# Expert outputs scattered into token order in place of gathers in the last phase

## The chip, the cores and the metric

One core of a Trainium2 chip runs the whole program in one launch. A NeuronCore has TensorE (PE), VectorE (DVE), ScalarE (ACT), GpSimd (POOL) and SyncE (SP), each with its own stream of instructions; they meet only at semaphores. 16 DMA engines carry the transfers. The metric is the device time of the program in microseconds.

## The reference

```python
x = layernorm(x + attention(x))         # (8, 1024, 256)
x = layernorm(x + ffn(x))

def ffn(x):                             # 8 experts, 2 chosen for each token
    gates = softmax(xf @ gate_w)
    topw, topi = top_k(gates, 2);  topw = topw / sum(topw)
    h = gelu(ln(einsum('td,edh->teh', xf, w1) + b1, ln1_g, ln1_b))
    y = einsum('teh,ehd->ted', h, w2) + b2
    out = einsum('ted,te->td', y, combine)    # combine: topw at the chosen experts, 0 elsewhere
    return ln(out + xf, ln_g, ln_b)
```

There are 8192 tokens of 256 features, a hidden size of 512, and so 16384 pairs of a token and a chosen expert. The attention (16 heads, latents of 32, rotary tables, causal) is computed first and is not touched by the change, but for the routing at the end of each batch.

## The kernel before

Phases follow each other: `weight_phase` folds weights, `attention_phase` does the attention batch by batch with the routing of each batch (the order of its items is written out by hand in `PLACES`), `expert_phase` runs the experts on gathered tiles of tokens, `combine_phase` mixes the two outputs of each token and normalises. Each phase ends with a barrier of all engines.

*Routing.* For each of the 8 batches, `route_step(b, i)`, i from 0 to 21 on VectorE, finds the two experts of each token (8 tiles of 128 tokens) and the token's place in each expert's list. The place is a number of a row in the DRAM table `token_of_row` (67584 rows: 8320 for each expert, and spare ones). Step 19 stores the places in `routes["slot"]`, step 20 the token numbers in `ids`. Then 16 indirect DMAs of GpSimd (items `SCAT`, L769) write the token numbers to the table, 128 elements of 4 bytes each. The table was filled with zeros in `weight_phase`.

*Tables at the end of the routing* (L879 to L919). VectorE works out for 136 tiles of 128 rows (`MAX_TILES`: 128 full tiles and one partial one for each expert) which expert and which first row of the table each has. The experts' outputs are kept tile by tile in DRAM, `y_rows` with 136 x 128 rows, so the places in `routes["slot"]` are corrected at last to rows of `y_rows` (L902 to L912), behind a wait for all scatters. `y_rows` holds padding rows as well.

*Expert stage* (`expert_phase`). It is pipelined over the tiles k by hand, each engine with its own order. SyncE loads 128 token numbers (`tok`, L1006) up to 12 tiles ahead, GpSimd gathers the 128 rows of x1 (L984, an indirect DMA) 6 tiles ahead. TensorE transposes them (L1047), ScalarE rounds them to fp32r (`x_hi`, L1093), VectorE takes the remainder (`x_lo`, L1104), and TensorE multiplies with w1 in three products of high and low halves (L1058). VectorE adds the bias (L1113), takes statistics (L1123 to L1127), GpSimd raises the variance to the power -1/2 (L990), VectorE normalises (L1118), TensorE transposes (L1024), ScalarE applies GELU (L1076) and rounds (`g_hi`, L1080, in two halves of two column blocks). The low halves `g_lo` are the remainders: those of blocks 0 and 1 are taken by VectorE (L1130) at the end of its turn, those of blocks 2 and 3 by GpSimd (L994). TensorE multiplies with w2 (L1036), ScalarE moves the result to SBUF (`y_out`, two buffers, L1087), and SyncE stores it as a plain block of `y_rows` (L1009).

*Last phase* (`combine_phase`). It goes over 16 groups of 512 tokens (`CG` = 4 tiles), with three buffers. SyncE loads x1 (0.5 MB) and stores the output (0.5 MB) of the group three before. GpSimd gathers both outputs of each token by `routes["slot"]`, 8 indirect DMAs of 128 rows a group (L1202), a group as soon as `mixed` says that the one three before was used. TensorE sums x1 and the two outputs times their weights (L1216, L1218, `f_ps`), VectorE and ScalarE do two layer norms (L1239 to L1277, L1327), and TensorE brings in x1 and a bias (L1227, L1228).

## Time and profile before

| | us |
|---|---|
| median of 3 runs (2500.8 to 2524.76) | 2509.27 |
| the profiled execution | 2506.28 |
| its span | 2504.6 |
| TensorE, VectorE, ScalarE, GpSimd busy | 2162.4, 1672.8, 1366.1, 1373.5 |

A row of a group of instructions has its line in the kernel, engine, operation, output <- input, and count, then the busy time, the mean of one in ns, and the idle time of the engine just ahead of them with what ended it. A row of the order of time begins with the start and the duration in us. "issue" or "remote" as a cause means that the profile shows nothing that ended the wait. The expert stage lies from 1744 to 2281 us of the span, the last phase behind it.

### The profile page before, as it was taken

Reading aid. Unit: us, or ns where it says so; the run is one execution under the profiler, and the core shown is the slowest. Engines: PE = TensorE matmul, PEld = TensorE weight load, DVE = VectorE, ACT = ScalarE, POOL = GpSimd, SP = SyncE. Lnnn points to the kernel's source line nnn. Section 1 sums busy time; section 2 is a strip of 40 time slices with the busy share of each in tenths; the row PEclk is TensorE's granted clock in tenths of the full one; section 3 lists DMA queues with packets and bytes.
Section 4 is the critical chain, followed back from the end, with each engine's and each line's share of the span. In section 5 each row is a group of like instructions: output and inputs, shape, how many; then the busy total and the mean of one; then the engine's idle time right before and its main releaser. Section 6 shows DMA issues by size and latency. Waiting matters only on the chain. (4 is left out here: it accounts for less than half of the span.)

```text
span 2504.6 us, 43646 instructions
## 1 busy us (share of the span) xinstructions
PE 2162.4 (86%) x12268; PEld 1490.6 (60%) x12268; DVE 1672.8 (67%) x4866; ACT 1366.1 (55%) x3316; POOL 1373.5 (55%) x1606
## 2 busy tenths in 40 slices
PE   2698998999899999899899899940999999996876
PEld 2454655555555555556556566430888888885665
DVE  2476687686577687677677678434777777773676
ACT  0155655555545565564564566621677777773333
POOL 1455465664654754763674675415566666665562
PEclk7799999998898898998998999865999999998898
DMA  3556556556545555564565565250222222223563
GB/s 116 129 123 146 120 119 155 113 120 142 124 100 133 118 130 136 120 136 120 125 131 128 119 128 129 49 199 7 65 71 71 71 71 70 70 71 105 158 185 114
DMA packets 192967, 284.06 MB, mean 113 GB/s; under 512 B 55752, under 2 KB 113760, under 8 KB 192608
## 3 DMA queue, kind: packets, MB, share of 16 engines
q1 hardware_dynamic: 173664, 238.18, 40.0%
q0 software_dynamic: 16768, 34.69, 4.8%
q10 hardware_dynamic: 2304, 8.39, 0.9%
q8 instruction: 110, 1.80, 0.3%
q14 instruction: 121, 0.99, 0.2%
HBM read 99.41 MB, written 37.56 MB: 55 GB/s over the span
## 5 line engine op out<-in xcount | busy, mean ns | idle before, releaser
L515 ACT ACTIVATE probs<-scores_T 128x512 f32<-128x512 f32 (+3 forms) x1536 | 654.5, 492 | 258.5 <-PE scores_T L405 245.9
L748 POOL TENSOR_SCALAR_AFFINE_SELECT probs<-probs 128x256 f32<-128x256 f32 x512 | 205.6, 410 | 544.4 <-ACT probs L515 541.7
L463 PE MATMUL ring<-k_stack,q_stack_b 96*128 96x512 f32 (+3 forms) x1024 | 403.5, 437 | 19.4 <-DVE neg_part L660 9.1
L660 DVE TENSOR_REDUCE neg_part<-ring 128x1 f32<-128x512 f32 x512 | 333.2, 683 | 96.5 <-PE ring L463 93.5
L405 PE MATMUL scores_T<-q_stack_b,k_stack 98*128 98x512 f32 (+3 forms) x1024 | 328.3, 398 | 46.5 <-ACT probs L515 45.8
L422 PE MATMUL o_ps<-probs,v_ones 128*17 128x512 f32 (+3 forms) x3072 | 350.7, 530 | 1.9 <-POOL probs L748 1.7
L463 PEld LDWEIGHTS ring<-k_stack,q_stack_b 96*128 96x128 f32 x1024 | 196.7, 201 | 228.9 <-issue 84.8
L665 DVE CUSTOM_DVE_ANT_0 ring<-ring,mask 128x384 f32<-128x384 f32 (+3 forms) x512 | 243.3, 507 | 116.7 <-PE ring L463 114.5
L665 DVE CUSTOM_DVE_ANT_0 ring<-ring,mask,neg_part 128x384 f32<-128x384 f32 (+3 forms) x512 | 260.7, 554 | 83.6 <-PE ring L463 83.3
L1076 ACT ACTIVATE o_sb<-ht_ps,ln_b,ln_g 128x128 f32<-128x128 f32 x544 | 217.1, 449 | 114.7 <-PE ht_ps L1024 76.4
L405 PEld LDWEIGHTS scores_T<-q_stack_b,k_stack 98*128 98x128 f32 x1024 | 193.3, 206 | 104.0 <-ACT probs L515 79.5
L445 PE MATMUL ring<-x_hi,lat_w 128*128 128x512 f32 x512 | 189.1, 412 | 29.4 <-DVE x_lo L637 29.4
L523 ACT ACTIVATE u<-ring,lat_bias 128x512 f32<-128x512 f32 x128 | 87.8, 688 | 205.3 <-PE ring L445 190.0
L463 PE MATMUL ring<-k_stack,q_stack_a 96*128 96x384 f32 (+3 forms) x512 | 172.3, 371 | 24.5 <-DMA k_stack<-u_rot 20.4
L732 POOL TENSOR_TENSOR u<-u,cos 128x512 f32<-128x512 f32 x128 | 164.6, 1286 | 40.4 <-DMA u_rot<-u 40.1
L990 POOL TENSOR_TENSOR h_rstd<-h_ve,minus_half 128x1 f32<-128x1 f32 x136 | 91.4, 672 | 173.1 <-DVE h_ve L1127 173.1
L740 POOL TENSOR_TENSOR u<-u,u_rot 128x512 f32<-128x512 f32 x128 | 164.6, 1286 | 9.7 <-POOL u_rot L735 0.4
L1036 PE MATMUL y_ps<-w_hi,g_hi 128*128 x544 | 165.6, 304 | 3.0 <-DVE g_lo L1130 1.5
L769 POOL DMA_INDIRECT token_of_row<-ids,slot x128 | 140.9, 1101 | 48.9 <-DVE ids_f L621 25.7
L735 POOL TENSOR_TENSOR u_rot<-u_rot,sin 128x512 f32<-128x512 f32 x128 | 166.2, 1298 | 0.1
L984 POOL DMA_INDIRECT z<-x,tok x136 | 137.4, 1010 | 41.4 <-issue 25.6
L1202 POOL DMA_INDIRECT y<-y_rows,slot x128 | 121.0, 946 | 67.1 <-issue 35.3
(192 smaller groups left out, 4682.2 us busy)
## 6 DMA issues: line engine op xcount, KB each, us to landing
u_rot<-u SPq DMA_DIRECT2D x128, 256.0 KB, 3.7
k_stack<-u_rot SPq DMA_DIRECT2D x128, 256.0 KB
y_rows<-z SPq DMA_DIRECT2D x136, 128.0 KB
lat_w<-lat_split SPq DMA_DIRECT2D x32, 512.0 KB
q_stack_a<-u_rot SPq DMA_DIRECT2D x64, 256.0 KB
q_stack_b<-u_rot SPq DMA_DIRECT2D x64, 256.0 KB
k_stack<-u SPq DMA_DIRECT2D x64, 256.0 KB
x_raw<-in_xT SPq DMA_DIRECT2D x16, 512.0 KB, 4.9
```

Of the source, the lines that this page charges most:

```text
L405: nc.tensor.matmul(sc[(t + j) % 3][:, HALF - w:HALF], k_stack[:, n % 2, h, P * kb:P * kb + P], q_stack[c][:, row_buf(n, c), h, q0 - HALF * ...
L422: last = nc.tensor.matmul(o_ps[32 * h:32 * h + VW, q0 - HALF * c:HALF], v_ones[:, b % 2, kb, HG * g + h, :], probs[:, s % 2, h, cols], sta ...
L445: last = nc.tensor.matmul(out[:], lat_w[:, kc, side, w_, :], a[:, kc, cols], start=i == 0, stop=i == 5)
L463: nc.tensor.matmul(out[:, 0:k1 - k0], q_stack[qb // 4][0:3 * L, row_buf(n, qb // 4), h, P * (qb % 4):P * (qb % 4) + P], k_stack[0:3 * L, n ...
L515: nc.scalar.activation(probs[:, s % 2, h, cols], sc[(t + j) % 3][:, HALF - w:HALF], ACT.Exp).then_inc(exp_done, 1)
L660: nc.vector.tensor_reduce(neg_part[:, n % 2, part_col], src[:], AX_X, ALU.max, negate=True).then_inc(max_taken, 1)
L665: nc.vector.tensor_tensor_reduce(out=src[:, 0:w], in0=src[:, 0:w], in1=consts["mask"][:, HALF - w:HALF], scale=-1.0, scalar=neg_part[:, n ...
L732: nc.gpsimd.tensor_tensor(u[s][:, cols], u[s][:, cols], consts["cos"][:, cols], ALU.mult).then_inc(cos_done[s], 1)
L735: nc.gpsimd.tensor_tensor(u_rot[s][:, cols], u_rot[s][:, cols], consts["sin"][:, cols], ALU.mult).then_inc(sin_done[s], 1)
L748: nc.gpsimd.affine_select(both, both, [[0, 2], [1, P]], ALU.is_ge, zero, base=0, channel_multiplier=-1).then_inc(kept, 1)
L1036: nc.tensor.matmul(y_ps[j % 2][:, 0:C], a[j % 2][:, f, :], experts[w][:, bass.ds(e, 1), C * f:C * f + C], start=f == 0 and a is g_hi and w ...
L1076: nc.scalar.activation(g[k % 2][:, f, :], ht_ps[k % 2][:, P * f:P * f + P], ACT.Gelu, bias=experts["ln1_b"][:, f, bass.ds(e, 1)], scale=ex ...
```

## The change

The row table has two numbers for each row: the token, and the row of the output table `y_rows`, which is now in token order: row t for the first choice of token t, 8192 + t for the second, and one more row, 16384, for all padding. The routing scatters both numbers. In the expert stage GpSimd scatters each tile's 128 result rows to these rows (two tiles later in its order, four buffers), and each scatter waits until the one before it has landed. SyncE no longer stores results there and only loads row numbers, up to 16 tiles ahead. VectorE takes both low halves: the first ahead of the statistics, the second behind them. The last phase loads y as plain blocks on SyncE, and GpSimd does nothing in it. The correction of the places goes, as do `routes["slot"]` and the tables it used.

```diff
-            nc.vector.memset(zero_ids[:], 0).then_inc(zero_set, 1)
+            nc.vector.memset(no_token[:, :, 0], 0).then_inc(zero_set, 1)
+            nc.vector.memset(no_token[:, :, 1], 2 * B * T).then_inc(zero_set, 1)
...
-                return nc.vector.tensor_copy(routes["slot"][:, :, TB * b:TB * b + TB], slot_f[:])
+                return nc.vector.tensor_copy(slot[:], slot_f[:])
...
-                    if i == 20 and n:
+                    if i == 19 and n:
                         dve.wait_ge(scattered, 16 * 2 * TB * n)
...
-                    j = TB * n + tb
                     nc.gpsimd.indirect_dma_start(
-                        token_of_row, bass.IndirectOffsetOnAxis(routes["slot"][:, k, j:j + 1], 0),
-                        ids[:, tb:tb + 1], None).then_inc(scattered, 16)
+                        token_of_row, bass.IndirectOffsetOnAxis(slot[:, k, tb:tb + 1], 0),
+                        ids[:, k, tb, :], None).then_inc(scattered, 16)
...
-                slots_by_expert = [P, 2 * TILES, E]
-                slots = routes["slot"][:].rearrange("p k t -> p (k t)")
-                then(nc.vector.tensor_copy(all_f[:], slots))
-                then(nc.vector.tensor_tensor(beyond, all_f[:].unsqueeze(2).to_broadcast(slots_by_expert),
-                                             next_base[:].unsqueeze(1).to_broadcast(slots_by_expert), ALU.is_ge))
-                then(nc.vector.tensor_tensor(beyond, beyond, delta[:].unsqueeze(1).to_broadcast(slots_by_expert),
-                                             ALU.mult))
-                then(nc.vector.tensor_reduce(skip[:], beyond, AX_X, ALU.add))
-                then(nc.vector.tensor_tensor(skip[:], all_f[:], skip[:], ALU.subtract))
-                dve.wait_ge(scattered, 16 * 2 * TILES)
-                nc.vector.tensor_copy(slots, skip[:])
...
-            for k in range(-6, MAX_TILES):
+            for k in range(-6, MAX_TILES + 2):
                 if tile(k + 6):
                     j = k + 6
-                    pool.wait_ge(tok_loaded[j % 8], 16 * (j // 8 + 1))
+                    pool.wait_ge(tok_loaded[j % 4], 16 * (j // 4 + 1))
                     if j >= 4:
                         pool.wait_ge(xt_full, j - 3)
                     nc.gpsimd.indirect_dma_start(x_in[j % 4], None, x1_rows,
-                                                 bass.IndirectOffsetOnAxis(tok[:, j % 8:j % 8 + 1], 0)
+                                                 bass.IndirectOffsetOnAxis(tok[:, j % 16, 0:1], 0)
                                                  ).then_inc(x_in_loaded[j % 4], 16)
                 if tile(k + 2):
                     j = k + 2
                     pool.wait_ge(ve_done, j + 1)
                     nc.gpsimd.tensor_tensor(h_rstd[j % 2][:], h_ve[j % 2][:], routes["minus_half"][:],
                                             ALU.pow).then_inc(rstd_done, 1)
-                if tile(k):
-                    pool.wait_ge(g_hi_ready, 2 * k + 2)
-                    nc.gpsimd.tensor_tensor(g_lo[k % 2][:, pairs[1], :], g[k % 2][:, pairs[1], :],
-                                            g_hi[k % 2][:, pairs[1], :].bitcast(F32),
-                                            ALU.subtract).then_inc(g_lo2_ready, 1)
+                if tile(k - 2):
+                    j = k - 2
+                    pool.wait_ge(y_ready, j + 1)
+                    if j:
+                        pool.wait_ge(y_stored[(j - 1) % 4], 16 * ((j - 1) // 4 + 1))
+                    nc.gpsimd.indirect_dma_start(y_rows, bass.IndirectOffsetOnAxis(tok[:, j % 16, 1:2], 0),
+                                                 y_out[j % 4], None).then_inc(y_stored[j % 4], 16)
+            for a in range(4):
+                pool.wait_ge(y_stored[a], 16 * (MAX_TILES // 4))
 
         @block.sync
         def _(sp):
-            for k in range(-12, MAX_TILES):
-                if tile(k + 12):
-                    j = k + 12
-                    row = sp.value_load(routes["row"][0:1, j:j + 1], min_val=0, max_val=ROWS - P)
-                    if j >= 8:
-                        sp.wait_ge(x_in_loaded[j % 4], 16 * (j // 4 - 1))
-                    sp.dma_start(tok[:, j % 8:j % 8 + 1], token_of_row[bass.ds(row, P), :]).then_inc(tok_loaded[j % 8], 16)
-                if tile(k):
-                    sp.wait_ge(y_ready, k + 1)
-                    sp.dma_start(y_rows[P * k:P * k + P, :], y_out[k % 2]).then_inc(y_stored[k % 2], 16)
-            for a in range(2):
-                sp.wait_ge(y_stored[a], 16 * HALF_TILES)
+            for j in range(MAX_TILES):
+                row = sp.value_load(routes["row"][0:1, j:j + 1], min_val=0, max_val=ROWS - P)
+                if j >= 4:
+                    sp.wait_ge(tok_loaded[j % 4], 16 * (j // 4))
+                if j >= 16:
+                    sp.wait_ge(y_stored[j % 4], 16 * (j // 4 - 3))
+                sp.dma_start(tok[:, j % 16, :], token_of_row[bass.ds(row, P), :]).then_inc(tok_loaded[j % 4], 16)
+            for a in range(4):
+                sp.wait_ge(tok_loaded[a], 16 * (MAX_TILES // 4))
...
-                        pe.wait_ge((g_lo_ready, g_lo2_ready)[i], j + 1)
+                        pe.wait_ge(g_lo_ready, 2 * j + i + 1)
...
-                    if j >= 2:
-                        act.wait_ge(y_stored[j % 2], 16 * (j // 2))
-                    nc.scalar.activation(y_out[j % 2], y_ps[j % 2][:, 0:C], ACT.Identity).then_inc(y_ready, 1)
+                    if j >= 4:
+                        act.wait_ge(y_stored[j % 4], 16 * (j // 4))
+                    nc.scalar.activation(y_out[j % 4], y_ps[j % 2][:, 0:C], ACT.Identity).then_inc(y_ready, 1)
...
+            def split_g(k, i):
+                part = pairs[i]
+                dve.wait_ge(g_hi_ready, 2 * k + i + 1)
+                nc.vector.tensor_tensor(g_lo[k % 2][:, part, :], g[k % 2][:, part, :],
+                                        g_hi[k % 2][:, part, :].bitcast(F32), ALU.subtract).then_inc(g_lo_ready, 1)
...
                                             h_rstd[j % 2][:, 0:1], ALU.subtract, ALU.mult).then_inc(h_norm_ready, 1)
+                if tile(k):
+                    split_g(k, 0)
...
                     nc.vector.tensor_scalar(h_ve[j % 2][:], h_mv[j % 2][:, 1:2], EPS, None, ALU.add).then_inc(ve_done, 1)
                 if tile(k):
-                    dve.wait_ge(g_hi_ready, 2 * k + 1)
-                    nc.vector.tensor_tensor(g_lo[k % 2][:, pairs[0], :], g[k % 2][:, pairs[0], :],
-                                            g_hi[k % 2][:, pairs[0], :].bitcast(F32),
-                                            ALU.subtract).then_inc(g_lo_ready, 1)
+                    split_g(k, 1)
...
                     sp.dma_start(x1[n % 3][:], tiles_of(x1_dram)[n]).then_inc(x1_loaded[n % 3], 16)
+                    for k in range(2):
+                        src = tiles_of(y_rows[B * T * k:B * T * (k + 1), :])[n]
+                        sp.dma_start(y[k][n % 3][:], src).then_inc(y_loaded[n % 3], 16)
...
-        @block.gpsimd
-        def _(pool):
-            for n in range(n_groups):
-                if n >= 3:
-                    pool.wait_ge(mixed, CG * (n - 2))
-                for t in range(CG):
-                    for k in range(2):
-                        nc.gpsimd.indirect_dma_start(
-                            y[k][n % 3][:, t, :], None, y_rows,
-                            bass.IndirectOffsetOnAxis(routes["slot"][:, k, CG * n + t:CG * n + t + 1], 0)
-                        ).then_inc(y_loaded[n % 3], 16)
...
-                pe.wait_ge(y_loaded[n % 3], 16 * 2 * CG * (n // 3 + 1))
+                pe.wait_ge(y_loaded[n % 3], 16 * 2 * (n // 3 + 1))
...
-    token_of_row = nc.dram_tensor("token_of_row", (ROWS, 1), I32).ap()
-    y_rows = nc.dram_tensor("y_rows", (MAX_TILES * P, C), F32).ap()
+    token_of_row = nc.dram_tensor("token_of_row", (ROWS, 2), I32).ap()
+    y_rows = nc.dram_tensor("y_rows", (2 * B * T + 1, C), F32).ap()
```

## Rows read from the trace of the kernel before

**Rows 1.** Busy time of each engine by stretch: expert stage, last phase.

```profile
core 0: us, PE busy (x) PEld busy (x) DVE busy (x) ACT busy (x) POOL busy (x), PEclk, DMA share, GB/s
1900.00:2250.00 350.00, 344.89 (x2297) 304.14 (x2296) 262.40 (x644) 264.77 (x736) 220.16 (x276) 1.00 0.25 71
...
2340.00:2400.00 60.00, 50.43 (x225) 41.78 (x224) 42.62 (x187) 25.47 (x75) 38.83 (x42) 1.00 0.59 178
```

**Rows 2.** Groups of instructions of the expert stage; first GpSimd's low half alone.

```profile
L994 POOL TENSOR_TENSOR g_lo<-o_sb,g_hi x136: 714/729/743, 1764.8 to 2276.4; 128x256 fp32r<-128x256 f32 x136
...
L984 POOL DMA_INDIRECT z<-x,tok x79 | 80.0, 1012 | 15.7 <-issue 15.7
...
L1130 DVE TENSOR_TENSOR g_lo<-o_sb,g_hi 128x256 fp32r<-128x256 f32 x79 | 32.9, 416 | 0.0
```

**Rows 3.** Order of time, one tile of the expert stage.

```profile
2031.40 0.60 PE L1024 MATMUL ht_ps<-ident,h_norm 128*128 128x128 f32 x4
...
2032.92 0.68 DVE L1123 BATCH_NORM_STATS2 h_stats<-h_norm 128x6 f32<-128x512 f32 x1
...
2032.99 0.42 ACT L1080 ACTIVATE g_hi<-o_sb 128x256 fp32r<-128x256 f32 x1
...
2034.99 0.60 PE L1024 MATMUL ht_ps<-ident,h_norm 128*128 128x128 f32 x4
```

**Rows 4.** Order of time, start of the last phase.

```profile
2290.55 0.95 POOL L1202 DMA_INDIRECT y<-y_rows,slot  x1 [0.30 <-issue]
...
2293.45 1.19 PE L1216 MATMUL f_ps<-x,ident 128*128 128x256 f32 x2 [14.97 <-DMA y<-y_rows,slot]
```

**Rows 5.** SyncE: last stores of the expert stage; its waits (total, times, longest).

```profile
2276.59 2.65 SPq L1009 DMA_DIRECT2D y_rows<-z  x2
...
SPq L375 <- DMA inv_sums<-inv: 106.5, 27, 7.5
...
SPq L1011 <- DMA y_rows<-z: 1.4, 1, 1.4
```

**Rows 6.** Order of time, end of the routing.

```profile
1708.82 11.42 DVE L720 TENSOR_TENSOR w_lo<-w_lo,w_hi 128x1024 fp32r<-128x1024 f32 x10
1708.84 12.38 POOL L769 DMA_INDIRECT token_of_row<-ids,slot  x1 [0.30 <-issue]
...
1731.61 0.96 POOL L769 DMA_INDIRECT token_of_row<-ids,slot  x1 [0.31 <-issue]
1742.50 0.23 DVE L912 CAST slot<-skip 128x128 int32<-128x128 f32 x1 [18.02 <-DMA token_of_row<-ids,slot]
...
1743.45 0.22 DVE L916 TENSOR_TENSOR weight<-weight,w_tmp 128x64 f32<-128x64 f32 x1
```

**Rows 7.** The last phase: a wait in total, the gathers' line, order of time.

```profile
DVE c_stats L1239 <- remote: 41.3, 10, 12.6
...
L1202 POOL DMA_INDIRECT y<-y_rows,slot x128: 940/946/1000, 2281.7 to 2464.3; - x128
...
2298.53 0.76 DVE L1239 BATCH_NORM_STATS2 c_stats<-f_ps 128x6 f32<-128x256 f32 x2 [16.93 <-issue]
...
2326.73 1.65 DVE L1268 SCALAR_TENSOR_TENSOR v<-v,c_rstd,xb_ps 128x256 f32<-128x256 f32 x4 [11.04 <-issue]
...
2363.65 0.94 POOL L1202 DMA_INDIRECT y<-y_rows,slot  x1 [1.99 <-remote]
...
2375.33 0.94 POOL L1202 DMA_INDIRECT y<-y_rows,slot  x1 [1.99 <-remote]
...
2468.15 1.66 DVE L1268 SCALAR_TENSOR_TENSOR v<-v,c_rstd,xb_ps 128x256 f32<-128x256 f32 x4 [9.44 <-issue]
...
2484.16 1.65 DVE L1262 SCALAR_TENSOR_TENSOR v<-f_ps,c_mv,ln_g_rep 128x256 f32<-128x256 f32 x4
...
2489.12 0.76 DVE L1239 BATCH_NORM_STATS2 c_stats<-f_ps 128x6 f32<-128x256 f32 x2
...
2492.80 1.65 DVE L1262 SCALAR_TENSOR_TENSOR v<-f_ps,c_mv,ln_g_rep 128x256 f32<-128x256 f32 x4
```

More of the change, by code:

```diff
@@ L79, in _ @@
                 sp.dma_start(dst[:], dram[name]).then_inc(loaded, 16)
-            sp.wait_ge(zero_set, 1)
-            sp.dma_start(token_of_row.rearrange("(p s) o -> p (s o)", p=P), zero_ids[:]).then_inc(zeroed, 16)
+            sp.wait_ge(zero_set, 2)
+            sp.dma_start(token_of_row.rearrange("(p s) o -> p s o", p=P), no_token[:]).then_inc(zeroed, 16)
             sp.wait_ge(split, 1)
@@ L194, in attention_phase @@
         before, ones, chosen, first, second = (tail[k] for k in ("before", "ones", "chosen", "first", "second"))
-        top, best, slot_f, ids_f, ids = (tail[k] for k in ("top", "best", "slot_f", "ids_f", "ids"))
+        top, best, slot_f, slot, ids_f, ids = (tail[k] for k in ("top", "best", "slot_f", "slot", "ids_f", "ids"))
         flat = lambda m: m.rearrange("p t e -> p (t e)")
@@ L956, in expert_phase @@
         g_lo = [sb(f"g_lo{a}", [P, FC, P], F32R) for a in range(2)]
-        y_out = [tail["z"][:, 4 + a, :] for a in range(2)]
+        y_out = [tail["z"][:, 4 + a, :] for a in range(4)]
         ps = lambda name: [ctx.enter_context(nc.psum_tensor(f"{name}{a}", [P, HALF], F32)) for a in range(2)]
         xt_ps, h_ps, ht_ps, y_ps = ps("xt_ps"), ps("h_ps"), ps("ht_ps"), ps("y_ps")
-        tok = sb("tok", [P, 8], I32)
-        tok_loaded = [sem(f"tok_loaded{a}") for a in range(8)]
+        tok = sb("tok", [P, 16, 2], I32)
+        tok_loaded = [sem(f"tok_loaded{a}") for a in range(4)]
         x_in_loaded = [sem(f"x_in_loaded{a}") for a in range(4)]
-        y_stored = [sem("y_stored0"), sem("y_stored1")]
+        y_stored = [sem(f"y_stored{a}") for a in range(4)]
         xt_full, xe_hi_ready, xe_lo_ready, h_full = sem("xt_full"), sem("xe_hi_ready"), sem("xe_lo_ready"), sem("h_full")
@@ L1070, in _ @@
                     if k >= 2:
-                        act.wait_ge(g_lo_ready, k - 1)
-                        act.wait_ge(g_lo2_ready, k - 1)
+                        act.wait_ge(g_lo_ready, 2 * (k - 1))
                         act.wait_ge(y_full, k - 1)
@@ L1367, in build @@
         sb = lambda name, shape, dt=F32: ctx.enter_context(nc.sbuf_tensor(name, shape, dt))
-        routes = {"ident": sb("ident", [P, P]), "weight": sb("weight", [P, 2, TILES]),
-                  "slot": sb("slot", [P, 2, TILES], I32)}
+        routes = {"ident": sb("ident", [P, P]), "weight": sb("weight", [P, 2, TILES])}
         tail = tail_buffers(ctx, nc)
```

17 lines of the change are left out of this document (8 added, 9 removed).

## The prediction

> **What bounds the kernel now.** I read the busy time by stage first [rows 1]. In the expert stage TensorE is busy 344.9 of 350 us and its clock is granted at 1.00 (2.4 GHz), while VectorE, ScalarE and GpSimd are at 63 to 76%. In the last phase no engine passes 85% (TensorE 50.4 of 60 us) and the DMA engines stand at 0.59. So the expert stage is bound by TensorE's stream and the last phase by something else.
>
> The groups of instructions of the expert stage [rows 2] give its beat: GpSimd's low half starts 136 times between 1764.8 and 2276.4, so a tile takes 511.6 / 135 = 3.79 us. The order of time inside one tile [rows 3] shows TensorE going from one set of transposes (2031.40) to the next (2034.99) in 3.59 us with no idle time, beside ScalarE and VectorE, which wait for it.
>
> The last phase is read from three places. In its middle GpSimd starts a batch of 8 gathers at 2363.65 and the next at 2375.33, a group every 11.68 us, and waits 1.99 us between batches [rows 7]. VectorE waits 41.3 us in all, in 10 waits, for something that the profile can't name, and twice more stands still, 11.04 and 9.44 us, just before 2326.73 and 2468.15 [rows 7]. Once the gathers are over (the last starts at 2464.3), the same code does a group in 2492.80 - 2484.16 = 8.64 us [rows 7]. The chain of waits, followed back, lies almost wholly in this phase.
>
> **The change, part by part.**
>
> *The last phase loses its 128 gathers.* From the first statistics of group 0 (2298.53) to those of group 15 (2489.12) it takes 190.6 us [rows 7]. Without gathers every group should go as the last ones do: 15 x 8.64 = 129.6 us, so **-61.0 us**. The bounds: at best this (the order of TensorE's and VectorE's instructions doesn't change), at worst the named waits stay and nothing is gained. I take the full sum because the unnamed waits and the two standstills all lie beside gathers and none lies behind the last one. Cover: the loads. A group moves x1, two y blocks and its output, 4 x 0.52 = 2.1 MB. At 178 GB/s the DMA engines are busy 0.59 [rows 1], which makes 302 GB/s at full share, so 6.9 us for a group, under 8.64. If that cover failed, a group would be bound by the transfers; at twice the cost per byte, 13.9 us, the phase would lose 32 us on before instead of winning.
>
> *Its start.* Now TensorE begins at 2293.45, 2.9 us behind the start of the eighth gather at 2290.55 [rows 4]. After, SyncE issues two 0.13 MB and three 0.52 MB loads, at about the time of the first gather, 2281.7 [rows 7]: 1.8 MB at 302 GB/s are 6.0 us, and about 2 us from issue to the last landing (the plain store takes 1.7 [rows 5]), so 2290: **-3.5 us** (bounds -6 and 0). SyncE then issues four DMAs a group in place of two; it waits for output n-3 before it loads n+1, which leaves two groups, 17 us, for a load.
>
> *Expert stage, the scatter.* SyncE's store of a tile goes, and GpSimd gets an indirect DMA; nothing of before writes 1 KB rows this way. For the issue I take a gather's 1.0 us [rows 2]. GpSimd is busy 220.2 of 350 us [rows 1], 2.38 us a tile; less the low half's 0.73 plus 1.0 that is 2.65, and with some 0.3 us ahead of each indirect DMA about 3.2 of 3.79. It fits. But a scatter isn't issued before the one ahead of it has landed, so the landing time L, from its start, sets a floor under the beat. Behind that wait stand the next tile's gather and the power that VectorE's normalisation waits for. The gather, on the same queue and with the same rows and bytes, lands in 2.9 us [rows 4]. The lower bound is the plain store, 0.3 + 1.4 = 1.7 us [rows 5]; the upper one the token scatter of 4-byte elements, whose last started at 1731.61 and freed VectorE at 1742.50, 10.9 us [rows 6]. I take 2.9, the row nearest in queue, row size and bytes: under 3.79, so **0** in the steady beat. With the upper end it would be 136 x 7.1 = +967 us.
>
> The Trainium skill, "DMA: Bandwidth & Descriptors", section "Anatomy of one DMA — SWDGE (gpsimd) path", gives about 2.0 us plus bytes / 436e3 for such a DMA; by an estimate from that page L would be 2.3 us and the term 0 as well, but its section puts most of the 2 us on the receipt of the target memory and calls HBM the heaviest, which speaks for more in this direction.
>
> *Expert stage, the low half.* GpSimd's 0.73 us becomes a second 0.42 us on VectorE [rows 2]. VectorE goes from 262.4 / 350 x 3.79 = 2.84 to 3.26 us a tile, 86%. The first one now stands ahead of the statistics: it must wait for ScalarE's rounding, which ends at 2032.99 + 0.42 = 2033.41, where the statistics started at 2032.92 [rows 3]. So statistics and everything behind them, the variance that GpSimd waits for included, come 0.5 + 0.4 = 0.9 us later. The normalisation, whose end the statistics followed at 2032.92, is over 2.0 us before the transposes that read it start at 2034.99 [rows 3], so these are not late: **0** (below: a gain of 0.05 us a tile at most, for TensorE has no more idle time [rows 1]; above: the second rival).
>
> *End of the expert stage.* The last two stores start at 2276.59 and about 2278.9, and the last is in 1.4 us behind 2279.24, at 2280.6 [rows 5]. Now the last scatter waits for the one before it: that can start at 2276.6, lands at 2279.5, and the last lands at 2282.4: **+2 us** (bounds 0 and, by the landing rival, 7). SyncE's token loads run up to 16 tiles ahead and stay hidden.
>
> *Routing.* After the last token scatter VectorE did a cast and three more steps, 1742.50 to 1743.67 [rows 6]; these run earlier now: **-1.2 us**. Five table steps on VectorE lay under the scatters: 0. The token scatter carries 8 bytes instead of 4, 128 descriptors either way: 0 taken, bounds -1 and +2. The wait that moves one step ahead is for scatters of the batch before, long over: 0. The zero table of twice the size lies beside the weight loads: 0.
>
> **The sum**: -61.0 - 3.5 + 2 - 1.2 = -63.7 us on the profiled execution's 2506.28 (span 2504.6 and 1.7 around it) gives 2442.6. The median of the runs is 3.0 above that execution, so 2446.
>
> **Rivals.**
>
> *Landing bound (slower).* The place is GpSimd's wait ahead of each scatter. For: stores to HBM of short rows in the attention stage let SyncE wait 106.5 us in 27 waits, 3.9 us each and up to 7.5, behind the issue [rows 5], and the token scatter took 10.9. With 0.95 of issue L is 4.9 us, the beat too, and the stage grows by 136 x 1.1 = 151 us: 2597. It decides from L = 3.79 + 63.7 / 136 = 4.26 us on. Against: those rows are 4 and 128 bytes, these 1 KB.
>
> *GpSimd and VectorE in each other's way (gain shrinks).* VectorE ran ten subtractions with both inputs in SBUF, 11.42 us from 1708.82; GpSimd's indirect DMA of 1708.84 took 12.38 us instead of 0.96 [rows 6]. The change puts two such subtractions a tile beside two indirect DMAs. If each blocks GpSimd for its 0.42 us, GpSimd needs 3.2 + 0.84 = 4.04 us, 0.25 over the beat: +34 us, 2480. Against: GpSimd idles before the power, so that blocks mostly eat idle time. The Trainium skill, "SBUF — State Buffer", section "Who interferes with whom", states that a VectorE instruction with two SBUF inputs and a GpSimd one that reads SBUF exclude each other. The trace agrees with it.
>
> *The last phase's waits stay.* The 1.99 us and the unnamed waits might come from the plain loads, which also end with the gathers. Then a group keeps some 3 us of waits: 15 x 3 = 45 us less gain, 2491. Against: GpSimd, which touches none of these loads, waits in the same places.
>
> **Numbers.** The forecast 0.62, its own range 2434 to 2462; landing bound 0.14; GpSimd against VectorE 0.14; waits stay 0.10. A 1% change is 25 us, about what a measurement tells from none. Faster by over 1% is the forecast, two thirds of the second rival and a third of the third: 0.62 + 0.09 + 0.03 = 0.74. Slower is the landing rival, 0.14. Within 1% is the rest, 0.12. The range reaches from 2434 (start and end of the phases at their good ends, a few us less in the last phase) to 2491, and leaves out the landing rival and part of the third, 0.19.
>
> **What would show it.** In the changed profile: the last phase at 8.6 us a group and without unnamed waits; the expert stage at 3.79 us a tile with GpSimd waiting little for its own scatters; statistics on VectorE starting right behind the first low half. A beat near the scatter's landing time, with GpSimd waiting for a DMA ahead of each scatter, would prove me wrong, as would a last phase with a busy share of the DMA engines near 1.

## The result and the profile after

The changed kernel takes **2413.88 us** in the median (2398.45 to 2421.28, 4 runs) beside 2509.91 for the kernel before (2500.8 to 2524.76, 4 runs) on the same chip: a ratio of 0.963 with the 95% interval 0.957 to 0.969. It is faster by 3.7%, and by 32 us more than I had forecast (2446). The time lies under my range, which began at 2434. The profiled execution took 2408.44 us, with a span of 2406.7. (Of the 11 runs of the kernel before beside experiments 5, 6 and 10, one ran at a granted clock of 0.80 in place of 0.91 to 0.93 and is left out of their range.)

These are the busy times by stage of the changed kernel, in the columns of [rows 1]:

```profile
1850.00:2200.00 350.00, 348.37 (x2383) 314.91 (x2382) 303.08 (x763) 276.00 (x765) 261.23 (x286) 1.00 0.25 74
2260.00:2320.00 60.00, 60.00 (x280) 52.82 (x279) 53.94 (x231) 28.57 (x85) 0.00 (x0) 1.00 0.69 218
```

In these 60 us of the last phase TensorE is now busy all of the time, on 280 products where there were 225, and GpSimd does nothing. In the expert stage TensorE's busy time rises by 3.5 us only, but the **number** of its instructions in 350 us rises from 2297 to 2383, by 3.7%. That is what I had not expected.

The next rows (line, engine, operation, tiles, count, shortest, median and longest in ns, first and last start) give the beat of the expert stage, the scatter and the statistics of the last phase:

```profile
L1118 DVE BATCH_NORM_STATS2 h_stats<-h_norm x136: 679/686/695, 1727.7 to 2220.4; 128x6 f32<-128x512 f32 x136
...
L984 POOL DMA_INDIRECT y_rows<-z,tok x136: 959/1057/1321, 1743.4 to 2237.9; - x136
...
L1222 DVE BATCH_NORM_STATS2 c_stats<-f_ps x64: 412/420/433, 2260.2 to 2392.6; 128x6 f32<-128x256 f32 x64
```

(2220.4 - 1727.7) / 135 = 3.65 us a tile, where the kernel before took 3.79 by [rows 2]. The end of the expert stage, in order of time, shows GpSimd's last scatters, ScalarE's last y_out and SyncE's first load of the last phase:

```profile
2228.50 0.38 ACT L1074 ACTIVATE z<-y_ps 128x256 f32<-128x256 f32 x1 [1.45 <-PE y_ps L1027]
...
2230.32 0.96 POOL L984 DMA_INDIRECT y_rows<-z,tok  x1 [2.98 <-DMA y_rows<-z,tok]
2234.02 0.96 POOL L984 DMA_INDIRECT y_rows<-z,tok  x1 [2.75 <-DMA y_rows<-z,tok]
2237.88 0.96 POOL L984 DMA_INDIRECT y_rows<-z,tok  x1 [2.90 <-DMA y_rows<-z,tok]
...
2246.44 0.35 SPq L1172 DMA_DIRECT2D ln_g_rep<-in_ln_g  x1
...
2254.92 1.19 PE L1199 MATMUL f_ps<-x,ident 128*128 128x256 f32 x2 [26.46 <-DMA y<-y_rows]
```

From the end of the last y_out, 2228.88, to the next phase it takes 17.6 us; in the kernel before it was 2.2 (2278.89 to 2281.10).

Where the 97.9 us between the two spans lie, by the same marks in both traces:

| stretch | before | after | difference | forecast |
|---|---|---|---|---|
| start to the first token scatter of the last batch | 1699.4 | 1678.5 | -21.0 | 0 |
| from there to the first x gather (routing) | 48.65 | 40.33 | -8.3 | -1.2 |
| to the last tile's h_norm transposes | 524.4 | 504.1 | -20.3 | 0 |
| to the end of the last y_out | 6.5 | 6.0 | -0.4 | 0 |
| to SyncE's first load of the last phase | 2.2 | 17.6 | +15.4 | +2 |
| to the first statistics | 17.4 | 13.8 | -3.7 | -3.5 |
| to the end | 206.1 | 146.5 | -59.6 | -61.0 |

All but the first row together, called "the rest" below, went from 805.2 to 728.2 us: -77.0, where I forecast -63.7.

### The profile page after: what moved, and what is told of

It reads as the page before. It is cut to its first block and busy times, and to the rows that moved or that the text cites. A ratio compares the mean times of both kernels' runs of the same rounds, so it can differ in the third digit from the quotient of the medians.

```text
span 2406.7 us, 43666 instructions
## 1 busy us (share of the span) xinstructions
PE 2111.4 (88%) x12268; PEld 1473.2 (61%) x12268; DVE 1718.2 (71%) x4997; ACT 1365.9 (57%) x3316; POOL 1302.6 (54%) x1478
## 5 line engine op out<-in xcount | busy, mean ns | idle before, releaser
L749 POOL TENSOR_SCALAR_AFFINE_SELECT probs<-probs 128x256 f32<-128x256 f32 x512 | 206.1, 411 | 529.1 <-ACT probs L516 526.1
L661 DVE TENSOR_REDUCE neg_part<-ring 128x1 f32<-128x512 f32 x512 | 333.5, 684 | 97.9 <-PE ring L464 94.8
L406 PE MATMUL scores_T<-q_stack_b,k_stack 98*128 98x512 f32 (+3 forms) x1024 | 321.0, 389 | 46.0 <-ACT probs L516 44.5
L423 PE MATMUL o_ps<-probs,v_ones 128*17 128x512 f32 (+3 forms) x3072 | 344.3, 522 | 1.8 <-POOL probs L749 1.6
L984 POOL DMA_INDIRECT y_rows<-z,tok x136 | 146.9, 1080 | 71.8 <-issue 28.2
L1024 PE MATMUL y_ps<-w_hi,g_lo 128*128 x544 | 154.0, 283 | 0.0
```

What stands on the lines that cost most here:

```text
L406: nc.tensor.matmul(sc[(t + j) % 3][:, HALF - w:HALF], k_stack[:, n % 2, h, P * kb:P * kb + P], q_stack[c][:, row_buf(n, c), h, q0 - HALF * ...
L423: last = nc.tensor.matmul(o_ps[32 * h:32 * h + VW, q0 - HALF * c:HALF], v_ones[:, b % 2, kb, HG * g + h, :], probs[:, s % 2, h, cols], sta ...
L661: nc.vector.tensor_reduce(neg_part[:, n % 2, part_col], src[:], AX_X, ALU.max, negate=True).then_inc(max_taken, 1)
L749: nc.gpsimd.affine_select(both, both, [[0, 2], [1, P]], ALU.is_ge, zero, base=0, channel_multiplier=-1).then_inc(kept, 1)
L1024: nc.tensor.matmul(y_ps[j % 2][:, 0:C], a[j % 2][:, f, :], experts[w][:, bass.ds(e, 1), C * f:C * f + C], start=f == 0 and a is g_hi and w ...
```

## The experiments

Medians on one chip are told beside the time of the kernel before on that chip. Since the attention phase ahead of it varies by tens of us from run to run, the rest of the profiled execution is the sharper number.

**1. Both low halves on VectorE, alone (e1).** What gave the faster beat? Where TensorE loses time in the kernel before is seen by its own starts, here in one tile, with GpSimd's work beside it:

```profile
2038.19 0.68 POOL L990 TENSOR_TENSOR h_rstd<-h_ve,minus_half 128x1 f32<-128x1 f32 x1 [1.56 <-DVE h_ve L1127]
2038.85 0.73 POOL L994 TENSOR_TENSOR g_lo<-o_sb,g_hi 128x256 fp32r<-128x256 f32 x1
...
2040.65 0.38 PE L1047 MATMUL xt_ps<-ident,z 128*128 128x128 f32 x2
2041.25 0.49 PE L1058 MATMUL h_ps<-w_hi,xe_hi 128*128 x1 [0.21 <-issue]
```

From the x transposes to the first W1 product it takes 0.60 us here and 0.17 in the tile before it (2036.98 to 2037.15). Only 0.21 us of it counts as idle, because the ends of products are modelled. The product's start lies 1.67 us behind the end of the low half, 2039.58. Of the 126 tiles between 1780 and 2260 us, 79 have such a gap of over 0.22 us (the others stand at 0.14 in the median), and in these 79 the product comes 1.66 us behind GpSimd's low half in the median. Together they lose 21 us. The edit on the kernel before:

```
-                if tile(k):                                # GpSimd
-                    pool.wait_ge(g_hi_ready, 2 * k + 2)
-                    nc.gpsimd.tensor_tensor(g_lo[k % 2][:, pairs[1], :], ...)
...
+                if tile(k):                                # VectorE, ahead of the statistics
+                    split_g(k, 0)
...
+                    split_g(k, 1)                          # behind them
```

> The kernel before with both low halves on VectorE and nothing else of the change. Theory A, late release: in the kernel before, 72 of 117 steady tiles let TensorE stand between its x transposes and the first W1 product (0.32 us there on average against a floor of 0.14), and that product comes 1.66 us behind the end of GpSimd's low half, so the low half, queued on GpSimd behind the power, is what TensorE's queue waits for. On VectorE it comes earlier: the beat falls from 3.79 to 3.60 to 3.66 us, the expert stage by 18 to 26 us, its end and the last phase stay as before, the time is 2484 to 2492. Theory B: the faster beat of the changed kernel comes from SyncE's order or from fewer stores; then the beat stays at 3.79 and the time at about 2510. Theory C, VectorE is late (86% busy): beat above 3.85, time above 2520.

2482.37 us beside 2509.02, ratio 0.989 (0.984 to 0.993); the rest is 777.2 us, -28.0. The beat, by the statistics' first and last start, is (2260.8 - 1774.7) / 135 = 3.60:

```profile
L1125 DVE BATCH_NORM_STATS2 h_stats<-h_norm x136: 680/686/696, 1774.7 to 2260.8; 128x6 f32<-128x512 f32 x136
```

Busy times in its expert stage, in the columns of [rows 1]:

```profile
1850.00:2200.00 350.00, 350.00 (x2427) 319.83 (x2426) 304.51 (x777) 280.14 (x778) 160.80 (x194) 1.00 0.26 75
```

2427 instructions in 350 us against 2297: TensorE now goes at the pace of the shortest tile of before, 3.59 us [rows 3], and 5 gaps are left, which lose 0.9 us in all. Theory A holds, with a little more gain than it named, and B and C fall: VectorE is at 87%, and the beat hasn't grown.

**2. The changed kernel with the low half back on GpSimd (e2).**

```
                 if tile(k + 2): ... power ...
+                if tile(k):
+                    pool.wait_ge(g_hi_ready, 2 * k + 2)
+                    nc.gpsimd.tensor_tensor(g_lo[k % 2][:, pairs[1], :], ...).then_inc(g_lo2_ready, 1)
                 if tile(k - 2): ... scatter ...
```

> The changed kernel with the second low half of each tile on GpSimd again, between the power and the scatter. Theory A: the beat goes from 3.65 back to 3.79 or more; GpSimd would have 0.96 + 0.68 + 0.73 + 1.06 us of work and about 0.2 ahead of each DMA, 3.9 us a tile, so 3.9 to 4.2, and the time rises by 35 to 75 us to 2450 to 2490. Theory B (the low half is not what made the beat faster): 3.60 to 3.66 and 2414.

2465.16 us (ratio 0.982, 0.980 to 0.985), the rest 765.5, +37.3 on the changed kernel. GpSimd, in order of time:

```profile
1951.32 1.06 POOL L989 DMA_INDIRECT y_rows<-z,tok  x1 [0.18 <-issue]
1952.68 0.97 POOL L971 DMA_INDIRECT z<-x,tok  x1 [0.30 <-issue]
1953.69 0.68 POOL L977 TENSOR_TENSOR h_rstd<-h_ve,minus_half 128x1 f32<-128x1 f32 x1
1954.35 0.72 POOL L981 TENSOR_TENSOR g_lo<-o_sb,g_hi 128x256 fp32r<-128x256 f32 x1
1955.24 1.06 POOL L989 DMA_INDIRECT y_rows<-z,tok  x1 [0.18 <-issue]
```

It waits for nobody and goes round in 1955.24 - 1951.32 = 3.92 us; the mean beat is 3.93. So with the scatter alone GpSimd would have been the bound, and the two edits belong together.

**3. The low half ahead of the power, still on GpSimd (e6).** The kernel before with these two exchanged:

```
+                if tile(k): ... low half ...
                 if tile(k + 2): ... power ...
-                if tile(k): ... low half ...
```

> The kernel before with two instructions of GpSimd exchanged: the second low half of tile k comes ahead of the power of tile k+2, and stays on GpSimd. Theory A (it is the time at which the low half ends, 1.66 us ahead of the first W1 product, that holds TensorE): ScalarE's rounding ends at about the same time as the variance, so the low half ends 0.65 us earlier; the largest stall is 0.46 us, so nearly all of them go: a beat of 3.60 to 3.65, the time 2482 to 2492. The power comes 0.7 us later, which VectorE's normalisation stands. Theory E (it is the engine: GpSimd's subtraction slows VectorE or the gather): the beat stays at 3.79, 2509.

2484.22 us beside 2506.74 (ratio 0.993, 0.988 to 0.998), the rest 787.5, -17.7. The beat is (2251.2 - 1753.6) / 135 = 3.69, half of the way and short of theory A's 3.60 to 3.65; TensorE's gaps fall from 21 us to 8. So an earlier end of the low half gives this half of the gain with the engine unchanged, and theory E, by which the beat stays, falls. What is left shows where the two engines start at once; first all 136 halves (shortest, median, longest in ns), then one tile in order of time:

```profile
L989 POOL TENSOR_TENSOR g_lo<-o_sb,g_hi x136: 731/803/1016, 1761.6 to 2258.5; 128x256 fp32r<-128x256 f32 x136
```

```profile
1949.43 0.41 DVE L1130 TENSOR_TENSOR g_lo<-o_sb,g_hi 128x256 fp32r<-128x256 f32 x1
...
1949.43 1.01 POOL L989 TENSOR_TENSOR g_lo<-o_sb,g_hi 128x256 fp32r<-128x256 f32 x1 [1.15 <-ACT g_hi L1080]
```

Beside VectorE's half GpSimd's takes up to 1.02 us in place of 0.73. All 38 halves of over 0.85 us overlap one of VectorE's, and 33 of the 44 tiles (of 126, counted as above) that still let TensorE stand come behind such a long half. That looks like the exclusion of my second rival, here between two subtractions; that it makes all of the stalls left is not shown. The Trainium skill, "SBUF — State Buffer", section "Who interferes with whom", says that a VectorE instruction with two SBUF inputs excludes a GpSimd one that reads SBUF; this trace agrees.

**4. The last phase without gathers, alone (e3).** The kernel before with two plain loads a group:

```
+                    for k in range(2):
+                        src = tiles_of(y_rows[B * T * k:B * T * (k + 1), :])[n]
+                        sp.dma_start(y[k][n % 3][:], src).then_inc(y_loaded[n % 3], 16)
...
-        @block.gpsimd
-        ...
```

> The kernel before, whose last phase loads two plain blocks of the expert results a group in place of 8 gathers (the rows are then in the wrong order, so its output is not the reference's); the expert stage is untouched. Theory A, the gathers made the waits: 8.6 to 8.8 us a group, the first to the last group's statistics in about 131 us in place of 190.6, the start 4 us earlier, together -63 us: 2444 to 2450. Theory B, the waits come from the plain loads or stores: 11 us a group or more, 2480 to 2510.

2438.86 us, ratio 0.974 (0.969 to 0.979); the rest 739.9, -65.3. From the first statistics to the end it takes 146.5 us as in the changed kernel, and the beat of the expert stage stays at 3.80. So without the gathers the last phase is that of the changed kernel: theory A. (About 2 us of the 65.3 are the routing's, 46.5 us here and 48.65 in the kernel before.)

**5. Half of the gathers (e9).** The first expert's rows gathered, the second's loaded:

```
+                    sp.dma_start(y[1][n % 3][:], tiles_of(y_rows[0:B * T, :])[n]).then_inc(x1_loaded[n % 3], 16)
...
-                    for k in range(2):
+                    for k in range(1):
                         nc.gpsimd.indirect_dma_start(y[k][n % 3][:, t, :], ...)
```

> The kernel before, whose last phase gathers only the first expert's rows (4 gathers a group) and loads the second's as one plain block a group (so rows in the wrong order, and its output is not the reference's). Theory A, GpSimd's queue is the last phase's bound: 8 x 1.25 = 10 us of issue and 1.7 of waiting make 11.68; with 4 gathers it is 5 and 1.7, 6.7, under TensorE's 8.64, and a group takes 8.6 to 8.9. Theory F, each gather holds the others up: half of the excess stays, 10.2 us a group.

2430.26 us in one run. GpSimd starts a group of four at 2336.59, 2345.23 and 2353.86: 8.64 us, TensorE's own pace, and the rest is 741.9. Theory A. This chip, however, was another than those before, and of a different kind, as the next runs show.

**6. The changed kernel again (e10), and the kernel before again (e12, e13).**

> The changed kernel once more, unaltered. Theory N, the attention phase's 21 us are chance: none of its instructions before the last batch's token scatter differ in a way that matters; in the traces of five kernels with the old routing code that scatter began between 1677.3 and 1719.5 us, in those of five with the new one between 1674.2 and 1706.6. What is left is 77 us behind that point, so the ratio is about 0.969 and the time 2425 to 2435 beside 2505 to 2510. Theory S, the attention phase gains too: the ratio is 0.963 or less.

2411.88 us (6 runs), but the kernel before took only 2460.79 in the median on this chip (2436.76 to 2469.52): a ratio of 0.980 (0.975 to 0.985). Neither theory had that. The rest of the changed kernel, 725.7 us, is as it was. Its attention phase ended at 1691.5, 13 us later than in the first trace of the same code.

> The kernel before, unaltered, for its trace. On one chip all its times were 2437 to 2470 us, on three others 2487 to 2525, while the changed kernel took 2394 to 2427 on that chip and 2398 to 2421 on the first. Something in the kernel before depends on the chip and has gone with the change. Theory L, it is the last phase with its 8 gathers a group (standstills of 9 to 11 us and waits that the profile can't name): on a chip where the time is under 2475, the phase from its first statistics on takes 165 to 185 us, on one where it is over 2485 it takes 200 to 206; the expert stage has a beat of 3.79 and the routing 46.3 to 48.7 us on either. Theory M, it is the attention phase: the last batch's token scatter begins before 1665 on a fast chip, and the last phase takes 205 us on all.

> The kernel before once more, unaltered, in the hope of the chip on which it took 2437 to 2470 us. Theory L: under 2475 us the last phase takes 165 to 185 us from its first statistics on, over 2485 us 200 to 206 us, beat and routing as ever. Theory M: the attention phase ends before 1665 on a fast chip and the last phase takes 205 us on all.

The first of the two fell on a slow chip (2504.14 us), the second on a fast one (2463.94). First and last gather and statistics on the fast one, then GpSimd in order of time there, then on the slow one:

```profile
L1202 POOL DMA_INDIRECT y<-y_rows,slot x128: 942/946/999, 2280.5 to 2439.3; - x128
L1239 DVE BATCH_NORM_STATS2 c_stats<-f_ps x64: 411/420/433, 2296.6 to 2448.1; 128x6 f32<-128x256 f32 x64
```

```profile
2329.29 0.94 POOL L1202 DMA_INDIRECT y<-y_rows,slot  x1 [0.30 <-issue]
2330.54 0.95 POOL L1202 DMA_INDIRECT y<-y_rows,slot  x1 [0.30 <-issue]
```

```profile
2345.74 0.95 POOL L1202 DMA_INDIRECT y<-y_rows,slot  x1 [0.30 <-issue]
2348.85 0.95 POOL L1202 DMA_INDIRECT y<-y_rows,slot  x1 [2.16 <-remote]
...
2357.62 0.95 POOL L1202 DMA_INDIRECT y<-y_rows,slot  x1 [0.30 <-issue]
2360.62 0.95 POOL L1202 DMA_INDIRECT y<-y_rows,slot  x1 [2.05 <-remote]
```

On the fast chip gather follows gather every 1.25 us without a break: 8 x 1.25 = 10.0 us a group, and 165.6 us from the first statistics to the end. On the slow one it is 11.77 (2348.85 to 2360.62), and 206.4. Beat (3.79 on both), routing (46.3 and 45.8) and attention (1700.7 and 1699.5) don't differ: theory L. So some 20 of the 40 us between the two are the waits of 2 us a group, and the rest two standstills of VectorE, 9.0 and 8.8 us, which the fast chip's trace hasn't. One slow chip was met twice, and stayed of its kind (2509.02 us, later 2521.48); what makes a chip of the one kind or the other is open.

> The kernel of the half gathers again (first expert's rows gathered, the second's loaded as plain blocks in the wrong order), for a chip on which the kernel before takes over 2485 us. On such chips its last phase shows 11.68 us a group and standstills, on the faster kind 10.0 us, GpSimd's 8 x 1.25. Theory A: with 4 gathers a group the queue of gathers has slack, late notices are covered, and a group takes 8.6 to 8.9 us on this kind of chip too. Theory R: the late notices go with every gather and hold up each group by 1 to 2 us whatever the queue: 9.6 to 10.7 us.

That was a fast chip once more (2439.96 us beside 2461.28). The same kernel again:

> The same kernel of the half gathers, still for a chip of the slower kind. Theory A: 8.6 to 8.9 us a group there too. Theory R: 9.6 to 10.7 us.

Now the kernel before took 2521.48 on the same chip, and the half gathers 2431.07. A group takes 8.63 us (2346.06 to 2354.69 to 2363.32), without one unnamed wait. What stands between the groups is 3.94 us in which GpSimd waits for TensorE. So the waits cost nothing once the queue of gathers has such a pause: theory A. Whether they are gone then or only covered by it is not shown.

**7. The width of the token rows (e5).** The kernel before with a two-column table:

```
-    token_of_row = nc.dram_tensor("token_of_row", (ROWS, 1), I32).ap()
+    token_of_row = nc.dram_tensor("token_of_row", (ROWS, 2), I32).ap()
...
-                        ids[:, tb:tb + 1], None).then_inc(scattered, 16)
+                        ids[:, tb, :], None).then_inc(scattered, 16)
```

> The kernel before with a row table of two columns (both hold the token), so that each token scatter writes 8 bytes a row in place of 4 and each token load reads 8; the gathers of the last phase and everything else stay. From the last token scatter to the first x gather it took 16.5, 14.1 and 14.3 us in the three kernels with 4-byte rows so far, and 8.0 to 8.2 in the three with 8-byte rows. Theory W, the width of the row: 4-byte rows land slowly; then about 10 us here (1.2 us of VectorE's last steps still lie in it). Theory O, the order: VectorE's wait with its steps behind it makes the difference; then 14 to 16 us as before. The expert stage keeps its beat of 3.79 in both.

2472.72 us in one run. From the last token scatter to the first x gather 7.9 us, theory W, and the routing 40.15 us in all:

```profile
1709.50 0.96 POOL L769 DMA_INDIRECT token_of_row<-ids,slot  x1 [0.30 <-issue]
...
1712.15 0.23 DVE L912 CAST slot<-skip 128x128 int32<-128x128 f32 x1 [9.79 <-DMA token_of_row<-ids,slot]
```

With 8 bytes a row the last scatter is in after 2.65 us, with 4 after 10.9 [rows 6].

**8. A scratch row for each row without a token (e4).** The edit on the changed kernel:

```
-            nc.vector.memset(no_token[:, :, 1], 2 * B * T).then_inc(zero_set, 1)
+            nc.gpsimd.iota(no_token[:, :, 1], pattern=[[1, ROWS // P]], base=2 * B * T,
+                           channel_multiplier=ROWS // P).then_inc(zero_set, 1)
...
-    y_rows = nc.dram_tensor("y_rows", (2 * B * T + 1, C), F32).ap()
+    y_rows = nc.dram_tensor("y_rows", (2 * B * T + ROWS, C), F32).ap()
```

> The changed kernel in which each row of the table that has no token names a scratch row of its own, in place of one row for all. Theory P, rows of padding that all write to one row land slowly: the last scatters land in 3.2 us each in place of 3.7 to 3.9 and the last one well under the 8.5 us that passed from its start to the next phase; the stretch from the last y_out on ScalarE to the next phase's first load falls from 17.5 us to 12 or less, and the time by 4 to 7 us. Theory Q, the tail is the two tiles by which the scatter lags and the chain of landings: 17 us stay, time 2412 to 2416.

2424.15 us, ratio 0.966 (0.963 to 0.969). The tail, from the end of the last y_out to the next phase, is 16.1 us; in the changed kernel it was 17.6 in the first trace and 16.2 in the second. GpSimd's last three scatters:

```profile
2252.90 0.96 POOL L988 DMA_INDIRECT y_rows<-z,tok  x1 [3.51 <-DMA y_rows<-z,tok]
2256.05 0.96 POOL L988 DMA_INDIRECT y_rows<-z,tok  x1 [2.18 <-DMA y_rows<-z,tok]
2259.21 0.96 POOL L988 DMA_INDIRECT y_rows<-z,tok  x1 [2.20 <-DMA y_rows<-z,tok]
```

They follow each other after 3.15 and 3.16 us. With one row for all padding the last two landings took 3.70 and 3.86 us in both traces of the changed kernel and 3.72 and 3.86 in experiment 2, and from the last start to the next phase it is 7.9 us here and 8.6 in those three. So the landing part of theory P holds, 0.5 to 0.7 us for each of these scatters. Its size doesn't: another landing took 4.47 us (2248.43 to 2252.90), and the tail is no shorter than in the second trace. For the time Q stands, though it came out 8 us over Q's numbers: the attention phase ended at 1701.1, and the rest, 726.0, is that of the changed kernel.

**9. No wait for the scatter before (e7), and SyncE waiting for the last (e8).** On top of experiment 8:

```
-                    if j:
-                        pool.wait_ge(y_stored[(j - 1) % 4], 16 * ((j - 1) // 4 + 1))
```

and for e8 on top of that:

```
-            for a in range(4):
-                pool.wait_ge(y_stored[a], 16 * (MAX_TILES // 4))
...
+            for a in range(4):
+                sp.wait_ge(y_stored[a], 16 * (MAX_TILES // 4))
```

> The changed kernel with a scratch row of its own for each row of the table without a token (so no two rows of any scatter coincide), and without GpSimd's wait for the scatter before: a scatter is issued as soon as its tile is ready. Theory T, the chain of landings makes part of the tail: the last scatter then starts at about the end of the last y_out, in place of 8 to 9 us later, and the tail falls from 17.6 or 16.1 to 8 to 10 us; the beat from 3.65 to 3.60 to 3.63. Together 8 to 13 us under e4: 2411 to 2416. Theory U, landings pile up: the scatters then land later each and the tail stays over 14 us.

> As e7, but the wait for the last scatters is SyncE's, and GpSimd ends its part of the phase behind the last issue. After the changed kernel's last scatter the DMA engines are idle from 2240.0 us on, and the next phase begins only at 2246.4. Theory G, GpSimd's own end of the phase takes some 5 us once its last wait is over: here it runs beside the landing and the tail falls by 2 to 4 us more than in e7. Theory H, the landing is told late: the same as e7 within 1 us.

Without the chain 2409.5 us (ratio 0.962, 0.956 to 0.968), with SyncE's wait 2399.96 (0.959, 0.954 to 0.964), beside 2506.74. The beat is 3.61 in both, the tail 8.1 and 6.4 us, the rest 712.6 and 711.0. In the trace of e7 the last scatter starts 0.3 us behind the end of the last y_out (2218.77), and the next phase 7.8 us later:

```profile
2219.05 0.96 POOL L986 DMA_INDIRECT y_rows<-z,tok  x1 [0.88 <-ACT z L1076]
...
2226.89 0.35 SPq L1174 DMA_DIRECT2D ln_g_rep<-in_ln_g  x1
```

So the chain of landings cost 8.7 us at the end (2237.88 against 2228.88 + 0.3) and 0.04 us a tile before it: theory T. Another 0.7 us of the tail is the last landing, on rows of its own (experiment 8). GpSimd's own end of the phase costs 1.7 us, under the 2 to 4 of theory G and over the 1 of theory H.

**10. The best version (e11).** On top of that, SyncE's loads of group 0 go ahead of the two norm vectors:

```
-            sp.dma_start(g_rep[:], dram["ln_g"]).then_inc(gb_loaded, 16)
-            sp.dma_start(b_rep[:], dram["ln_b"]).then_inc(gb_loaded, 16)
...
+                    if n == 0:
+                        sp.dma_start(g_rep[:], dram["ln_g"]).then_inc(gb_loaded, 16)
+                        sp.dma_start(b_rep[:], dram["ln_b"]).then_inc(gb_loaded, 16)
```

> As e8 (scratch rows for padding, no wait for the scatter before, SyncE waits for the last scatters), and in the last phase SyncE loads x1 and the two y blocks of group 0 ahead of the two vectors of the norm. In the changed kernel the y block is issued 1.3 us after SyncE's first load and lands 6.5 us later, and TensorE starts on it. Theory A, the landing follows the issue: TensorE starts 0.8 to 0.9 us earlier in the phase, and the time is 17 to 20 us under the changed kernel's: 2405 to 2415. Theory D, the DMA engines are full with the five loads: no gain at the start.

2398.42 us (6 runs) beside 2411.88 for the changed kernel on the same chip; against the kernel before 0.977 (0.973 to 0.982) and 0.980 (0.975 to 0.985). These intervals overlap; the rest, 709.9 against 725.7, shows 15.8 us, nearly all of it experiment 9's (711.0). TensorE starts 7.5 us behind SyncE's first load, 8.35 in e8 and 8.5 in the first trace of the changed kernel: theory A, though the gap of the medians, 13.5 us, is under its 17 to 20.

## Why the prediction was wrong

The miss by the two profiled executions is 97.9 - 63.7 = 34.2 us: 21.0 from the attention phase, 20.3 from the expert stage's beat and 7.1 from the routing on the one side, 13.4 from the stage's end on the other; the other rows give back 0.8.

**The last phase (-61.0) and its start (-3.5)** were right in mechanism and size: -59.6 and -3.7, and a group at 2391.26 - 2382.63 = 8.63 us. What I could not see in one trace is that 40 of these 60 us belong to a kind of chip: on the other kind the gathers cost only their queue, 10.0 us a group, and the last phase would have won 165.6 - 146.5 = 19 us. That the forecast came out here is so in part luck: it was compared on a chip of the kind that its trace came from. I had taken the unnamed waits into the sum because none lay behind the last gather. That reading held, also on the slow kind with half of the gathers. One bound was miscounted: at 13.9 us a group 15 groups would have lost 15 x 13.9 - 190.6 = 18 us, not 32.

**The low half, "0 (below: a gain of 0.05 us a tile at most, for TensorE has no more idle time)"**, is the step that failed. The term is mis-sized: alone it gains 0.19 us a tile, 27.0 us from the first x gather to the last transposes (experiment 1), and 20.3 in the changed kernel, where the scatters take some back. I bounded it by TensorE's idle time, 350 - 344.9 us [rows 1]. But the ends of its products are modelled and overlap the next starts: a product of 0.28 us is followed by the next after 0.12. So a gap can grow by some 0.2 us before it counts as idle; in the tile of experiment 1 0.43 us are lost and 0.21 counted. The two numbers that tell it stood in my own text: a tile of 3.59 us [rows 3] and a mean of 3.79 [rows 2]. The difference times 136, 27 us, was the bound. The Trainium skill, "Perfetto Trace Analysis", section "Tensor Engine Instruction (MATMUL, LD_WEIGHTS)", calls TensorE's reported end an estimate from the instruction's size; the starts in the tile above agree.

**The scatter in the steady beat (0)** was nearly right. My L of 2.9 us is 3.2 in the trace where scatters follow at once (2219.90 to 2223.14, the next scatter waiting for the one before), under the beat; but in 12 of the tiles before these the next scatter waited 3.9 to 5.0 us for it, over the beat. It cost 0.04 us a tile, 6 us in the stage. The landing rival is out; it decided at 4.26.

**The end of the expert stage (+2, upper bound 7)** is the second failed step: +15.4. I counted one scatter behind the last y_out. There are three, since GpSimd takes tile k-2 in round k and the last tiles come faster than the beat (2.8 and 1.8 us) while a landing still takes 3.2 to 4.0. So the last scatter starts 9.0 us late, and 8.6 us pass from its start to the next phase, where I had allowed 2.9. Of these 8.6, 1.7 are GpSimd's end (experiment 9), 0.7 the shared padding row (experiment 8) and some 3.2 a landing; the 3 us left have no shown cause.

**Routing (-1.2)** came to -8.3, and the reason is not mine. The steps behind VectorE's wait brought nothing, and GpSimd's end seems to have taken their place: the next phase's first load comes 5.7 us behind the last scatter's start in the changed kernel and 5.4 in experiment 7, where VectorE still does them. The gain is the landing of the wider rows (experiment 7), which I had taken as 0 between -1 and +2. Some 2 of the 8.3 us are the trace's own: seven of the eight other traces with 4-byte rows take 45.8 to 46.7 us and one 48.2, where this one took 48.65.

**The attention phase** lies outside the sum: -21.0 us. Its end varied between 1677.3 and 1719.5 us in ten traces with the old routing code (mean 1695.8) and between 1674.2 and 1706.6 in seven with the new (mean 1686.9), so most of the 21 us is chance. What differs is TensorE's granted clock over that phase: 0.905 in the kernel before and 0.918 in the changed one. Over all 17 traces the phase's end follows it, from 1719.5 us at 0.883 (experiment 1) to 1674.2 at 0.921 (e7), and at like clocks old and new code agree: 1677.3 and 1685.9 at 0.915 and 0.916 (e5, e15), 1681.7 and 1678.5 at 0.915 and 0.918 (e8, the changed kernel). A line through the 17 leaves -1.4 us, with an error of 1.6, for the new code. So these traces show no gain there; why the clock differs from run to run is open.

**The rivals.** Landing bound: out. GpSimd against VectorE: the exclusion exists (experiment 3) but costs the changed kernel nothing that shows, since without the chain its beat is 3.61, beside 3.60 without any scatter. Waits that stay: out.

Without the attention phase's share I would have been 77.0 - 63.7 = 13 us off, at 2433, still just under my range: its lower end had room for the phases' ends, and none for a gain in the expert stage.

## What to carry to other kernels

For an engine whose ends are modelled, take the floor of a beat from the shortest tile and the loss from the mean beat, not from its busy share; then look for the gap between two starts that grows, and for what ended a fixed time ahead of it. A chain of indirect DMAs, each waiting for the one before, is free while its landing fits under the beat, and is paid for at the end by every one that is still queued. A gain that rests on waits without a name should be measured on more than one chip.

## What the runs showed of the hardware

- A token scatter of 128 rows of 4 bytes landed 10.9 us behind its start (7.95 to 10.4 in eight other traces), one of 8 bytes 2.65 us (one trace); a scatter of 128 rows of 1 KB landed in 3.2 us where the next waited for it, at times in up to 5.0. Where padding rows all went to one row, the last two took 3.70 and 3.86 us in place of 3.15.
- TensorE's first W1 product came 1.66 us after a late release of the low half, although from the first of the seven products and two transposes in between to that W1 product it takes only 0.97 us when the release is early. A register load and the addresses that hang on it lie between; that these are the reason is not shown.
- With gathers queued without a break, some chips (five traces) let GpSimd wait 2 us a group and VectorE stand still twice, for 7.7 to 19.4 us; the one trace of the kernel before on the other kind of chip has neither. With half of the gathers both kinds took 8.6 us a group.
- A phase whose last wait is GpSimd's ended 1.7 us later than one whose last wait is SyncE's (tail 8.1 us in e7, 6.4 in e8 and e11).
- A GpSimd subtraction of 0.73 us took up to 1.02 us beside a VectorE one with two SBUF inputs.
